# Cross-attention scores of a decoder layer as three float32r passes of split keys and queries, and the queries' turn moved into their own rows' PSUM bank

## What is computed

```python
q = x @ Wq.T                      # 32 heads of 16
k_raw, v_raw = context @ Wk.T, context @ Wv.T
kv = concatenate([k_raw, v_raw], -1).reshape(b, m, 32, 16, 2)
k, v = kv[..., 0], kv[..., 1]     # the pairs are interleaved
q, k = rmsnorm(q), rmsnorm(k)     # over the 16 elements of a head
scores = einsum('bhnd,bhmd->bhnm', q, k) * 16 ** -0.5
attn = softmax(scores, -1)
x = x + einsum('bhnm,bhmd->bhnd', attn, v)
```

## Time and profile before

| | |
|---|---|
| median of 3 runs | 937.76 us |
| the profiled execution | 936.51 us, its span 934.7 us |
| busy: TensorE, VectorE, ScalarE, GpSimd | 98%, 64%, 50%, 22% |
| cross-attention's 48 steps | about 411 to 700 us of the span |
| granted TensorE clock in them | 1.00 of 2.4 GHz |

### The profile page before, as it was taken

How to read it: one execution, slowest core, us unless ns; L and a number is a source line. 1 busy time by engine, 2 the same in 40 slices (tenths; PEclk the granted TensorE clock), 3 DMA queues, 4 the chain that set the end, 5 groups by cost and what they waited for, 6 DMA issues and landing times.

```text
span 934.7 us, 17966 instructions
## 1 busy us (share of the span) xinstructions
PE 911.8 (98%) x7198; PEld 794.8 (85%) x7198; DVE 597.8 (64%) x1300; ACT 467.5 (50%) x1113; POOL 202.6 (22%) x146
## 2 busy tenths in 40 slices
PE   8989999999999999999999999999999999999995
PEld 8989999999999998877787777777788887999995
DVE  6886666666665635674655655545458866888883
ACT  5533333333343334646656666667675334565651
POOL 0133333333333314401101001011000710223222
PEclk9999999999999999999999999999999999999998
DMA  6010090202011203140201001010032785998983
GB/s 219 24 68 23 2 335 6 88 17 76 27 65 38 76 2 121 60 136 1 80 12 35 13 23 35 3 34 13 1 125 74 242 241 196 353 307 270 308 214 45
DMA packets 31330, 93.60 MB, mean 100 GB/s; under 512 B 6176, under 2 KB 9488, under 8 KB 29328
## 3 DMA queue, kind: packets, MB, share of 16 engines
q1 hardware_dynamic: 26944, 83.27, 26.0%
q0 software_dynamic: 4304, 9.19, 5.0%
HBM read 73.80 MB, written 16.81 MB: 97 GB/s over the span
## 4 chain that ended last, share of the span: by engine, by line
PE 89%; DVE 6%; ACT 2%; issue 1%; DMA 1%; POOL 0%; SPq 0%; DVEq 0%
PE bank L556 24%; PE bank L557 23%; PE bank L558 23%; PE bank L811 3%; PE bank L828 3%; PE bank L657 3%; PE bank L632 2%; PE bank L778 1%; PE bank L644 1%; PE bank L925 1%; PE bank L838 1%; PE bank L673 1%; PE bank L933 1%; DVE kT L1829 1%; DMA xa<-x 1%
## 5 line engine op out<-in xcount | busy, mean ns | idle before, releaser
L1303 ACT ACTIVATE ee<-bank 125x448 f32<-125x448 f32 x192 | 91.0, 547 | 22.0 <-PE bank L811 21.0
L556 PE MATMUL bank<-wkv_hi,ctx_hi 128*125 128x512 f32 x192 | 80.2, 418 | 2.7 <-DVE kn L1820 2.1
L1548 DVE TENSOR_TENSOR E_lo<-F,E_hi 128x940 fp32r<-128x940 f32 (+3 forms) x62 | 80.5, 1322 | 3.5 <-ACT E_hi L1075 2.8
L2222 POOL TENSOR_TENSOR ctx_lo<-ctx_f,ctx_hi 128x500 fp32r<-128x500 f32 x24 | 30.4, 1267 | 219.6 <-ACT ctx_hi L1075 219.6
L557 PE MATMUL bank<-wkv_hi,ctx_lo 128*125 128x512 f32 x192 | 76.0, 396 | 0.0
L558 PE MATMUL bank<-wkv_lo,ctx_hi 128*125 128x512 f32 x192 | 75.7, 394 | 0.0
L1829 DVE COPY kT<-bank 128x250 f32<-128x250 f32 x48 | 20.1, 418 | 84.4 <-PE bank L778 84.3
L556 PE MATMUL bank<-wv_hi,xT_hi 128*112 128x256 f32 x256 | 72.7, 284 | 0.1
L558 PE MATMUL bank<-wv_lo,xT_hi 128*112 128x256 f32 x256 | 71.8, 280 | 0.0
L557 PE MATMUL bank<-wv_hi,xT_lo 128*112 128x256 f32 x256 | 71.7, 280 | 0.0
L2222 POOL TENSOR_TENSOR wqk_lo<-wqk_f,wqk_hi 128x1024 fp32r<-128x1024 f32 x14 | 33.7, 2405 | 174.6 <-ACT wqk_hi L1075 174.6
(11 more groups left out here) (391 smaller groups left out, 2608.1 us busy)
## 6 DMA issues: line engine op xcount, KB each, us to landing
F<-wexp SPq DMA_DIRECT2D x14, 1408.0 KB, 8.0
F<-wexp SPq DMA_DIRECT2D x14, 768.0 KB
wqk_f<-wqk SPq DMA_DIRECT2D x16, 512.0 KB, 4.2
ctx_f<-ctx SPq DMA_DIRECT2D x24, 250.0 KB, 2.7
slots<-zt SPq DMA_DIRECT2D x1, 5397.0 KB, 22.9
xg<-slots SPq DMA_DIRECT2D x21, 256.0 KB, 6.7
wv_f<-wv SPq DMA_DIRECT2D x8, 512.0 KB, 5.5
wo_f<-wo SPq DMA_DIRECT2D x8, 512.0 KB, 3.6
```

The lines of the kernel that those rows point to most:

```text
L556: e.matmul(out, a[0], b[0], start=first, stop=False)
L1303: e.activation(ee[(4 * n + r) % 8][:, :], SX[r][0:MS, 0:4 * T], ACT.Exp, scale=0.25).then_inc(*x_exped.did((n, r)))
L1548: return e.tensor_tensor(out, src, high.bitcast(F32), ALU.subtract)
L2222: return e.tensor_tensor(out, src, high.bitcast(F32), ALU.subtract)
```

## The change

Keys and queries are kept as a high and a low float32r part, and each score matmul in float32 becomes three in float32r that add up in the same bank: high x high, low key x high query, high key x low query, each pass for all four row tiles before the next. `k_copy` gets a second, dependent instruction (the low part, 128x250), `q_copy` two more (the low part for the even and the odd head, 128x224 each). The queries are turned into columns 256 to 479 of the bank in which they were projected, no longer into bank 7; the next item of that bank waits for `q_copied` as well. That item is projected in the step with m = 2.

```diff
@@ -207,17 +207,21 @@
         kn = [sbl(f"kn{i}", [MS, 256], F32, "wv") for i in range(2)]
         vb = [sbl(f"vb{i}", [MS, XH, VW], F32, "wv" if i < 2 else "mid") for i in range(6)]
         assert room["wv"][0] == place_w + 2 * KC * D * 4 + 2 * XH * 64 * 4
-        kT = [sbl(f"kT{i}", [128, 2, MS], F32, "mid") for i in range(6)]
+        kT = [[sbl(f"kT{i}_hi", [128, 2, MS], F32R, "mid")] for i in range(6)]
         assert room["mid"][0] == place_v
         ctx += [pairl(f"ctx{i}", [128, KC, MS], "mid") for i in (2, 3)]
         assert room["mid"][0] <= place_v + NB * 256 * 4
         ee = [sbl(f"ee{i}", [MS, 4 * T], F32, "mid" if i < 6 else "z") for i in range(8)]
-        qT = [sbl(f"qT{i}", [128, 2, 2, T], F32, "mid") for i in range(2)]
+        qT = [[sbl(f"qT{i}_hi", [128, 2, 2, T], F32R, "mid")] for i in range(2)]
         oo = [sbl(f"oo{i}", [128, 4 * T], F32, w) for i, w in enumerate(("mid", "mask"))]
         ss = [sbl(f"ss{i}", [MS, XH], F32, "free") for i in range(2)]
         rr = [sbl(f"rr{i}", [MS, XH], F32, "free") for i in range(2)]
         rq = [sbl(f"rq{i}", [MS, XH], F32, "free") for i in range(2)]
         half = sbl("half", [128, 2], F32, "free")
+        for i, where in enumerate(("free", "wv", "wv", "z", "z", "z")):
+            kT[i].append(sbl(f"kT{i}_lo", [128, 2, MS], F32R, where))
+        for i, where in enumerate(("mid", "z")):
+            qT[i].append(sbl(f"qT{i}_lo", [128, 2, 2, T], F32R, where))
         zz = sbl("zz", [T, XH, 16], F32, "wv")
         zc = sbl("zc", [T, XH], F32, "wv")
         gw_f = sbl("gw_f", [128, KC, NE], F32, "wv")
@@ -337,14 +341,12 @@
                 return ("n", 2, b + 1) if b + 1 < NB else None
             return (("n", 3, b - 1) if i == 2 else ("g", b - 1, i + 1)) if b else None

-        tx_uses = [("t", keys[0]), ("t", keys[1]), ("n", 2, 0), ("t", keys[2]), ("t", (0, "q"))]
+        tx_uses = [("t", keys[0]), ("t", keys[1]), ("n", 2, 0), ("t", keys[2])]
         for n in range(NK):
             if aside(n):
                 tx_uses += [aside(n)]
             if n + 3 < NK:
                 tx_uses += [("t", keys[n + 3])]
-            if n % MC == 1 and n // MC + 1 < NU:
-                tx_uses += [("t", (n // MC + 1, "q"))]
         tx_turn = len(tx_uses)
         tx_uses += [("o", NU - 1), ("n", 3, NB - 1), ("g", NB - 1, 5), ("g", NB - 1, 6)]
         TX, tx_before, tx_last = {}, {}, {7: ("p", 1), 3: ("s", 1)}
@@ -352,6 +354,7 @@
             i = 3 if n >= tx_turn else 7
             TX[u], tx_before[u], tx_last[i] = banks[i], tx_last[i], u
         KB, SX, AB = banks[0:2], banks[2:6], banks[6]
+        QT = [KB[at_item[u, "q"] % 2][:, 256:256 + 2 * T] for u in range(NU)]

 
         jobs = [("s", j) for j in range(3)] + [(kd, q) for q in range(NP - 1) for kd in "po"] + [("o", NP - 1), ("p", NP - 1)]
@@ -483,7 +486,7 @@
         ctx_hi, ctx_lo = sig("ctx_hi", range(NB * MC)), sig("ctx_lo", range(NB * MC))
         kb_full, summed, rooted = (sig(n, items) for n in ("kb_full", "summed", "rooted"))
         squared = sig("squared", [(it, p) for it in items for p in ("sq", "v") if it[1] != "q" or p == "sq"])
-        kn_done, tx_full = sig("kn_done", items), sig("tx_full", tx_uses)
+        kn_done, tx_full, q_turned = sig("kn_done", items), sig("tx_full", tx_uses), sig("q_turned", range(NU))
         q_copied, k_copied = sig("q_copied", range(NU)), sig("k_copied", keys)
         KR = [(n, r) for n in range(NK) for r in range(4)]
         scored_x, x_exped, valued = sig("scored_x", KR), sig("x_exped", KR), sig("valued", KR)
@@ -731,6 +734,8 @@
             def kb_wait(n):
                 if n > 1:
                     w.wait_ge(*kn_done[items[n - 2]])
+                    if items[n - 2][1] == "q":
+                        w.wait_ge(*q_copied[items[n - 2][0]])
                 else:
                     v = kb_last[n]
                     w.wait_ge(*(pj_act if by_act(v) else pj_dve)[v])
@@ -764,19 +769,23 @@
                     w.wait_ge(*(gl_done if v[2] == 5 else lg_done)[v[1]])
                 elif v[0] == "o":
                     w.wait_ge(*z_scaled[v[1]])
-                elif v[1][1] == "q":
-                    w.wait_ge(*q_copied[v[1][0]])
                 else:
                     w.wait_ge(*k_copied[v[1]])

             def rows_turn(it):
                 n, u = at_item[it], ("t", it)
-                R = T if it[1] == "q" else MS
                 w.wait_ge(*kn_done[it])
                 tx_free(tx_before[u])
                 for g in range(2):
-                    i = e.transpose(TX[u][:, g * R:(g + 1) * R], kn[n % 2][0:R, g * 128:(g + 1) * 128], ident[0:R, 0:R])
+                    i = e.transpose(TX[u][:, g * MS:(g + 1) * MS], kn[n % 2][0:MS, g * 128:(g + 1) * 128], ident[0:MS, 0:MS])
                 i.then_inc(*tx_full.did(u))
+
+            def queries_turn(u):
+                n = at_item[u, "q"]
+                w.wait_ge(*kn_done[u, "q"])
+                for g in range(2):
+                    i = e.transpose(QT[u][:, g * T:(g + 1) * T], kn[n % 2][0:T, g * 128:(g + 1) * 128], ident[0:T, 0:T])
+                i.then_inc(*q_turned.did(u))

             def norm_turn(which, b):
                 u = ("n", which, b)
@@ -806,12 +815,15 @@
                 else:
                     for i in range(2, 6):
                         w.wait_ge(*pj_dve[pj_last[i]])
+                k, q = kT[n % 6], qT[u % 2]
                 for g in range(2):
-                    for r in range(4):
-                        i = e.matmul(SX[r][0:MS, g * 2 * T:(g + 1) * 2 * T], kT[n % 6][32 * r:32 * r + 32, g, :],
-                                     qT[u % 2][32 * r:32 * r + 32, g, :, :], start=True, stop=True)
-                        if g:
-                            i.then_inc(*scored_x.did((n, r)))
+                    for p, (a, b) in enumerate(((0, 0), (1, 0), (0, 1))):
+                        for r in range(4):
+                            at_ = slice(32 * r, 32 * r + 32)
+                            i = e.matmul(SX[r][0:MS, g * 2 * T:(g + 1) * 2 * T], k[a][at_, g, :], q[b][at_, g, :, :],
+                                         start=p == 0, stop=p == 2)
+                            if g and p == 2:
+                                i.then_inc(*scored_x.did((n, r)))

             def value_pe(n):
                 u, m = keys[n]
@@ -858,12 +870,14 @@
                     rows_turn(keys[n + 3])
                 value_pe(n)
                 if m == 1 and u + 1 < NU:
-                    rows_turn((u + 1, "q"))
+                    queries_turn(u + 1)

             def gu_wait(u):
                 v = gu_before[u]
                 if v[0] == "kn":
                     w.wait_ge(*kn_done[v[1]])
+                    if v[1][1] == "q":
+                        w.wait_ge(*q_copied[v[1][0]])
                 elif v[0] == "oo":
                     w.wait_ge(*oo_done[v[1]])
                 elif v[0] == "tx":
@@ -1024,7 +1038,7 @@
             rows_turn(keys[2])
             rows_pe(0, "q")
             o_pe(last, (4, 5))
-            rows_turn((0, "q"))
+            queries_turn(0)
             o_pe(last, (6,))
             rows_turn(keys[3])
             for n in range(NK):
@@ -1814,7 +1828,8 @@
                 e.scalar_tensor_tensor(y, tmp, 1.5, y, ALU.add, ALU.mult).then_inc(*own.step())
                 w.wait_ge(*own.last())
                 if n > 1:
-                    w.wait_ge(*tx_full["t", items[n - 2]])
+                    v = items[n - 2]
+                    w.wait_ge(*(q_turned[v[0]] if v[1] == "q" else tx_full["t", v]))
                 if m != "q":
                     w.wait_ge(*squared[(u, m), "v"])
                 e.tensor_tensor(kn[n % 2][0:R, :].rearrange("p (h d) -> p h d", d=16),
@@ -1826,18 +1841,23 @@
                 w.wait_ge(*tx_full["t", (u, m)])
                 if n > 5:
                     w.wait_ge(*scored_x[n - 6, 3])
-                e.tensor_copy(kT[n % 6][:, :, :], TX["t", (u, m)][:, 0:2 * MS].rearrange("p (g t) -> p g t", g=2)).then_inc(
-                    *k_copied.did((u, m)))
+                src, k = TX["t", (u, m)][:, 0:2 * MS].rearrange("p (g t) -> p g t", g=2), kT[n % 6]
+                e.tensor_copy(k[0][:, :, :], src).then_inc(*own.step())
+                w.wait_ge(*own.last())
+                low(k[1][:, :, :], src, k[0][:, :, :]).then_inc(*k_copied.did((u, m)))

             def q_copy(u):
-                w.wait_ge(*tx_full["t", (u, "q")])
+                w.wait_ge(*q_turned[u])
                 if u > 1:
                     w.wait_ge(*scored_x[MC * (u - 2) + MC - 1, 3])
                 w.wait_ge(*half_set[0])
-                e.tensor_tensor(qT[u % 2][:, :, :, :],
-                                TX["t", (u, "q")][:, 0:2 * T].rearrange("p (g t) -> p g t", g=2).unsqueeze(2).to_broadcast([128, 2, 2, T]),
-                                half[:, :].unsqueeze(1).unsqueeze(3).to_broadcast([128, 2, 2, T]), ALU.mult).then_inc(
-                    *q_copied.did(u))
```

(8 more changed lines are left out.)

## The result

The changed kernel takes **952.97 us** (median of 4 runs, 952.87 to 954.45) against 937.31 for the kernel before beside it (936.56 to 938.03): ratio 1.0171, 95% interval 1.0153 to 1.0188, 15.7 us slower. The forecast was 952.5.

What follows compares the result with a forecast made beforehand. TensorE was taken as bound by VectorE's chains at hand-overs without margin. Terms 6.3 + 9.65 + 0.4 - 1.5 = +14.85 us on the profiled 936.51, with 1.25 for the median, gave 952.5 us; range 945.5 to 963.5.

Steps and rivals of the forecast that it cites:

- What bounds: Cross-attention: in m = 1 steps TensorE's next rows start 0.06 us behind the end of VectorE's kn, so no margin.
- Term 1: Scores on TensorE: six rounds of 0.113 us make 0.89 a step, a gain of 0.08.
- rival A: Scores on TensorE: weight loads don't hide behind the round before; scores 1.45, total 963.3 us; 12%.
- Term 2: VectorE's keys' chain: the dependent low part makes kn 0.45 us later in 14 m = 1 steps, 6.3 us.
- Term 3: m = 2 steps: rows wait for the queries' low parts, 0.55 us in 8 steps, 0.75 in 7; sum with keys' 9.65.
- Term 4: Elsewhere: the scores' gain of 0.08 us is kept in 19 steps, 1.5 us; first scores start 0.4 later.
- Rival B: Cross-attention: TensorE's own order covers VectorE's added work, only the passes' gain counts; 934.0 or 928.2 us; 7%.
- Rival C: Scores on TensorE: float32r row tiles don't run side by side; scores 2.6 us, total 1013 us; 4%.
- rival D: Whole kernel: dependent instructions are cheaper and waits mostly coincide with others; change within 0.2%; 3%.

Runs made afterwards that it cites:

- e1: Changed kernel with all three passes taking the high parts and no low part made: 931.83 us, ratio 0.9936.
- e11: Kernel of e7 with the sums of the next keys, in steps with m = 0, moved ahead of VectorE's wait for the keys' turn: 929.92 us.
- e10: Changed kernel with the three passes of one row tile behind each other before the next tile's: 953.19 us, ratio 1.0171.
- e12: Changed kernel with all six passes of one row tile, both groups, behind each other before the next tile's: 974.88 us, ratio 1.0411.
- e5: Changed kernel with rows_sum of the next keys placed between the keys' high copy and their low part on VectorE: 946.89 us, ratio 1.011.
- e3: Changed kernel with only the keys' low part made and used, the third pass multiplying the high queries again: 940.73 us.
- e9: Changed kernel with the queries' turn back in bank 7 and no wait on queries ahead of the rows: 961.91 us, ratio 1.0259.
- e7: Changed kernel with the edits of e5 and e6, and the third norm moved ahead of the keys' copy: 932.59 us, ratio 0.9952.
- e6: Changed kernel with turned queries first copied out of their bank by one more VectorE instruction, TensorE's next rows waiting for that copy alone: 942.94 us.

## Why the prediction was right

**What bounds** held: the idle time of an engine lies in one place and its chain in another. Against the 98% and 64% of the earlier trace rows it was the 0.06 us between `kn` and the rows that told; e1 and e11 show that `kn` set the start there.

**Term 1, the passes:** 0.89 forecast, 0.85 measured; a round is 0.11 as taken from the values (0.113), not 0.093. The bound of 1.45 (rival A, with the rule on weight loads in the Trainium skill, TensorE: Matmul & The Clock Gate, Part 3) is refuted for float32r too: in e10, e12 and the changed kernel rounds in the same four row groups are 0.11 apart, less than the 0.206 of load and stream behind each other. The Trainium skill (TensorE: Matmul & The Clock Gate, LDWEIGHTS) gives columns / 1.2 ns for a load, as an estimate 104 ns for 125 columns. The 0.11 between rounds fits that; the record of a single load lasts 0.18 here.

**Term 2, the keys' low part:** 14 x 0.45 = 6.3 forecast; m = 1 lost 6.25 in all: 6.49 in the 14 (0.44 to 0.48 each, and 0.55 in one), less 0.11 and 0.13 gained in the first and in the last unit's. e5 and e3 show it by order and alone.

**Term 3, the queries' chain:** 9.65 forecast, 11.51 measured in 15 steps. The step that was mis-sized is the duration of a low part of the queries: taken as 0.39, from its width alone, it is 0.45, and the two 0.81 instead of 0.70. The two kinds of step then lose 0.66 and 0.87 instead of 0.55 and 0.75.

The prediction also held that the old place of the turn would have cost 0.45 a third time; e9, which has it, shows 0.19 in a step with m = 1.

**Term 4, the rest:** 1.5 forecast as a gain in 19 steps, about 2.0 measured there (1.80 in the 16 steps with m = 0, some 0.12 in each of two more; the last has no successor); 0.4 at the start, 0.5 measured.

**The sum:** 14.85 forecast, 15.96 + 0.5 = 16.5 booked from the traces, 15.7 between the medians. The mechanism and the counts were right; that the forecast is within 0.5 us of the result is in part luck. Term 3 was 1.9 too small and term 2 0.2, the gain of term 4 0.5 too small, which leaves the booked sum 1.6 above the forecast. The medians differ by 0.8 less than the booked sum, and the kernel before was 0.45 faster beside the changed one (937.31) than the 937.76 that the forecast started from. Rival B (VectorE is covered) is what e7 makes true by moving work: 932.6, where B had 934.0. Rival C fell with the 0.11 of a round, rival D with the ratio of 1.0171.

## What to carry to other kernels

Where two engines run in lockstep, read the margin at each hand-over from the two timelines; the waits list only margins already lost, and the kernel before had fourteen steps with a margin of nothing, of which the waits listed two. Price added work on the less busy engine by what stands behind it in its queue: here the low parts cost 21 us over e1 in one order, and 0.8 in another, with one copy more and the norm moved (e7). A buffer that another engine waits for should be emptied by the shortest instruction that does it (e6), and what nobody waits for yet, such as a low part needed three steps later, goes behind what is waited for (e5).

## What the runs showed of the hardware

- Float32r in row tiles of 32 rows: four tiles run side by side, one round of 125 by 224 columns every 0.11 us, against 0.19 for one of the two rounds that a float32 matmul takes. Three passes cost 0.85, one of float32 0.97.
- In the records TensorE starts matmuls of other row tiles ahead of earlier ones in its stream: three in a row for one tile don't delay the next tile (e10, 0.85 to 0.87), six do (e12, 1.81). The Trainium skill (TensorE: Matmul & The Clock Gate, Part 3) says that matmuls start in strict program order; the records of e10 differ, and its time, 953.19 us where the stream's order would have given an estimated 991, agrees with the records.
- Of seven waits of 1.5 us between dense matmuls in e9, three were followed by a granted clock of 1.2 GHz and four were not.
- A VectorE instruction with a scalar operand for each partition (128x224 out of PSUM) took 0.45 us; a plain copy of the same 128x224 out of PSUM took 0.39 (e6, into `qf`).
